# Attention and a LoRA mixture of experts: the products with V in three groups per head pair, of three, three and two key blocks, in place of four groups of two

## What is computed

```python
xq, xk, xv = x @ wq.T, x @ wk.T, x @ wv.T            # 16 heads of 32
scores = einsum("bqhd,bkhd->bhqk", xq, xk)
out = einsum("bhqk,bkhd->bqhd", softmax(scores), xv)
x = layernorm(x + out @ wo.T)
...
logits = x @ Wr.T + br
h = einsum("nd,erd->ner", x, A); y = einsum("ner,eor->neo", h, B) / 64
x = layernorm(x + y[argmax(logits)] * max(softmax(logits)))
```

## Time and profile before

| | us |
|---|---|
| median of 3 runs | 1507.79 |
| lowest and highest | 1507.14, 1510.0 |
| the profiled execution | 1506.31 |
| its span, from first to last instruction | 1504.5 |

### The profile page before, as it was taken

One profiled execution on the slowest core, in us unless ns is written; L12 is line 12 of the kernel. 1 busy time (PEld: TensorE's weight loads), 2 busy tenths in 40 slices (PEclk: granted clock), 3 DMA queues, 4 the chain that ended last, 5 costly groups with the idle time before them and its releaser, 6 DMA issues.

```text
span 1504.5 us, 21331 instructions
## 1 busy us (share of the span) xinstructions
PE 1444.2 (96%) x7176; PEld 909.3 (60%) x7176; DVE 976.8 (65%) x1850; ACT 784.7 (52%) x1430; POOL 1143.6 (76%) x651
## 2 busy tenths in 40 slices
PE   7999999999999999999999999999999999999997
PEld 5745556666645666666555666666664565565376
DVE  6747666666566677665556667666556777775564
ACT  3455556655455456455555546545554555555332
POOL 0376879888887779887779888879777899999311
PEclk9999999999999999999999999999999999999999
DMA  7345736574443434345353435234464112220001
GB/s 225 99 139 149 229 95 190 162 218 120 148 169 105 128 100 120 99 148 192 95 185 106 141 106 147 66 106 142 132 162 156 39 44 60 65 51 23 22 1 57
DMA packets 93661, 178.37 MB, mean 119 GB/s; under 512 B 19680, under 2 KB 35056, under 8 KB 92656
## 3 DMA queue, kind: packets, MB, share of 16 engines
q1 hardware_dynamic: 70240, 133.46, 31.2%
q10 hardware_dynamic: 22976, 42.47, 8.2%
q0 software_dynamic: 336, 1.07, 0.3%
HBM read 119.30 MB, written 56.88 MB: 117 GB/s over the span
## 4 chain that ended last, share of the span: by engine, by line
PE 82%; DVE 7%; issue 5%; POOL 3%; DMA 2%; ACT 1%; SPq 1%; ACTq 0%; POOLq 0%; DVEq 0%
PE w L697 24%; PE pv L856 15%; PE sc L844 14%; PE mx L834 13%; PE w L741 6%; DVE mxc L1156 3%; PE mx L808 3%; POOL Psum L596 2%; PE mx L697 1%; PE mx L768 1%; PE w L749 1%; DMA qk_parts<-split 1%; PE sc L697 1%; PE mx L757 1%; DVE stats L1245 1%
## 5 line engine op out<-in xcount | busy, mean ns | idle before, releaser
L1156 DVE TENSOR_REDUCE mxc<-mx 128x1 f32<-128x512 f32 x1024 | 682.7, 686 | 399.3 <-PE mx L834 396.6
L1001 ACT ACTIVATE P<-sc 128x512 f32<-128x512 f32 x1024 | 602.1, 597 | 483.9 <-PE sc L844 461.9
L596 POOL TENSOR_TENSOR Psum<-Psum,P 128x1024 f32<-128x1024 f32 x286 | 674.2, 2386 | 26.6 <-ACT P L1001 24.9
L844 PE MATMUL sc<-stack 98*128 98x512 f32 x1024 | 461.8, 453 | 5.8 <-ACT P L1001 4.9
L834 PE MATMUL mx<-stack 96*128 96x512 f32 x1024 | 406.9, 402 | 11.6 <-DVE eq L1295 4.9
L844 PEld LDWEIGHTS sc<-stack 98*128 98x128 f32 x1024 | 193.6, 189 | 97.0 <-issue 36.2
L834 PEld LDWEIGHTS mx<-stack 96*128 96x128 f32 x1024 | 195.1, 191 | 89.9 <-issue 27.6
L856 PE MATMUL pv<-P,V 128*32 128x512 f32 x2048 | 249.0, 604 | 0.0
L593 POOL TENSOR_TENSOR Psum<-P 128x1024 f32<-128x1024 f32 x50 | 118.8, 2392 | 114.4 <-ACT P L1001 88.8
L697 PE MATMUL w<-xT_s,wqk_s 128*128 128x512 f32 x504 | 161.5, 412 | 10.8 <-DVE xT_s L1172 10.8
L856 PEld LDWEIGHTS pv<-P,V 128*32 128x32 f32 x2048 | 56.6, 110 | 128.0 <-issue 102.4
(11 more groups left out here) (172 smaller groups left out, 1270.1 us busy)
## 6 DMA issues: line engine op xcount, KB each, us to landing
stack<-qk_parts SPq DMA_DIRECT2D x186, 256.0 KB, 4.4
qk_parts<-split SPq DMA_DIRECT2D x56, 512.0 KB, 3.5
wqk_s<-wqk_parts SPq DMA_DIRECT2D x40, 512.0 KB, 4.1
den_s<-den_parts SPq DMA_DIRECT2D x124, 64.0 KB, 2.0
r_f<-x ACTq DMA_DIRECT2D x3, 2048.0 KB, 12.6
wide<-a_parts ACTq DMA_DIRECT2D x3, 2048.0 KB, 8.0
out<-r_f SPq DMA_DIRECT2D x12, 512.0 KB, 3.4
xT_s_f<-xT ACTq DMA_DIRECT2D x5, 1024.0 KB, 8.3
```

What stands on the lines that cost most here:

```text
L596: pool.tensor_tensor(sums(s)[:, i, :], sums(s)[:, i, :], P[:, unit % NP, :], ALU.add).then_inc(add_done, 1)
L844: pe.matmul(sc[c][:, :], stack(s, i)[0:KS, 0, 128 * kb:128 * kb + 128], stack(s, i)[0:KS, 1, 512 * c:512 * c + 512], start=True, stop=True ...
L1001: act.activation(P[:, unit % NP, 512 * c:512 * c + 512], sc[c][:, :], ACT.Exp).then_inc(exp_done, 1)
L1156: dve.tensor_reduce(mxc[:, q % 2, at:at + 1], BANK["max", g][:, :], AX.X, ALU.max).then_inc(mx_done, 1)
```

## The change

The function that gives the blocks of a half is replaced by a table over the half in the slot: blocks 0, 1 and 2 at half 12, blocks 3, 4 and 5 at half 24, and, as before, blocks 6 and 7 at half 3 of the next slot (written as 35 of its own). The products, their operands and their semaphores stay. The groups of 12 and 24 stand in the first half of a unit, those of 11 and 19 stood in the second. Where `second` changes from one slot to the next, `den_at` goes from 11 to 12 (slots 25 to 28, 30 and 31); where it was 11 because of s % PAIRS == 2 alone (slots 10 and 18) it stays at 11. The steps at fixed distances from it follow.

```diff
--- before.py
+++ after.py
@@ -218,12 +218,14 @@
     def den_at(s):
 
 
-        return 6 if s <= PAIRS or s % PAIRS == 5 else 11 if second(s) != second(s - 1) or s % PAIRS == 2 else 3
-
-
-    def blocks(s, k):
-
-        return ((k - 5) // 2, (k - 3) // 2) if k % 4 == 1 and k >= 5 else ()
+        return 6 if s <= PAIRS or s % PAIRS == 5 else 12 if second(s) != second(s - 1) else 11 if s % PAIRS == 2 else 3
+
+
+    GROUPS = {12: (0, 1, 2), 24: (3, 4, 5), HALVES + 3: (6, 7)}
+
+    def blocks(h):
+
+        return GROUPS.get(h, ())
 
 
 
@@ -880,19 +882,17 @@
                     max_t(s + 1)
                 if s and half % HALVES == den_at(s):
                     den(s - 1, 0)
-                if c == 1 and s:
-                    for kb in blocks(s - 1, UNITS + k):
-                        if kb < KB:
-                            out_block(s - 1, kb)
-                if c == 1:
-                    for kb in blocks(s, k):
-                        out_block(s, kb)
+                if s:
+                    for kb in blocks(HALVES + half % HALVES):
+                        out_block(s - 1, kb)
+                for kb in blocks(half % HALVES):
+                    out_block(s, kb)
                 if half in X_PASS:
                     xi(*X_PASS[half])
                 for kind, n, chunk in AT.get(half, ()):
                     bank = begin((kind, n), False) if chunk == 0 else BANK[kind, n]
                     KIND[kind](n, chunk, bank)
-            for kb in blocks(LAST, UNITS + 1):
+            for kb in blocks(HALVES + 3):
                 out_block(LAST, kb)
             pe.wait_ge(exp_done, 2 * UNITS * SLOTS)
             pe.wait_ge(mx_done, max(FREES.values()))
```

## The result

The changed kernel takes 1521.71 us (median of 4 runs, 1519.79 to 1522.82), the kernel before on the same chip 1507.47 (4 runs, 1504.99 to 1510.0). The ratio is 1.0086, 95% interval 1.0066 to 1.0107: 13 us slower, where 6.7 us faster was forecast. The profiled execution of after is 1521.56, span 1519.8; before's was 1506.31, span 1504.5. The mean granted clock is 0.984 of full speed in after's trace and 0.993 in before's.

A forecast was written before the change was run, and what follows sets the result against it. The prediction took TensorE to set the pace. Its terms (-11.5 + 0.7 + 2.2 + 2.5 + 1.2 - 1.0 - 0.8) gave -6.7 us on 1506.31, 1499.6, or 1501.1 as median; range 1495 to 1506.5.

The forecast's parts named there:

- (a): TensorE: three groups a slot instead of four, each saving 0.36 us of entering and leaving narrow products, -11.5 us.
- rival F: TensorE's groups: the 0.36 us belongs to blocks, not groups, so that saving falls away; 1512.6 us, chance 0.02.
- (b): Dens of slots 10 and 18 stand alone at half 11, +0.7 us; in six other slots they stay joined.
- (c): New waits inside or behind the moved groups, on exponentials, buffers and V's tiles: cost nothing.
- (g): Group at 24 lets VectorE catch up before the maxima's transpose at half 26, -1.0 us.
- (h): Slots 15 and 23, halves from 24 on: longer group in front fills part of TensorE's waits, -0.8 us.
- (d): Chain over GpSimd gets shorter time, so dens of slots 9, 14 and 22 wait longer, +2.2 us.
- Rival D: GpSimd becomes the bound through the den in ten slots, 12.1 us instead of 2.2; 1511.0 us, chance 0.08.
- (e): Maximum banks: logit and transposed tiles lose the cover of groups at 19 and 27, net +2.5 us.
- (f): Slot 3, x passing through the maximum banks, loses the time the group at 19 gave VectorE, +1.2 us.
- Rival C: VectorE starves under groups of 2.91 us, holding at most three banks of work; 1505.4 us, chance 0.15.
- Rival E: Clock: waits of slots 9 and 14 grow and one more slow stretch costs 1.6 us; 1502.7, chance 0.03.

The follow-up runs named there:

- b2: Kernel before with reciprocals' store ahead of the stack load, maxima's transpose at half 24, and LEAD 5 for 4: 1506.29 us, ratio 0.998.
- best2: Changed kernel with reciprocals' store ahead of the stack load, maxima's transpose at half 24 before the group, and LEAD 5 for 4: 1496.94 us, ratio 0.9923.
- k24: Kernel before with only its third group moved, blocks 4 and 5 at half 24 instead of 27: 1523.51 us, ratio 1.0115.
- sp: Changed kernel with the reciprocals' store ahead of the stack load where both fall on half 14: 1517.83 us, ratio 1.0052.
- g27s: g27 with the reciprocals' store issued ahead of the stack load: 1506.49 us, ratio 0.998.
- g27: Changed kernel with its second group cut in two, block 3 at half 24, blocks 4 and 5 back at 27: 1518.06 us, ratio 1.0081.
- bsp: Kernel before with the reciprocals' store issued ahead of the stack load: 1504.35 us, ratio 0.9955.
- b24: Kernel before with the maxima's transpose at half 24 instead of 26, from slot 2 on: 1520.05 us, ratio 1.0102.
- best: Changed kernel with the maxima's transpose inside the group at half 24, behind block 3, and reciprocals' store ahead of the stack load: 1501.31 us, ratio 0.9936.

## Why the prediction was wrong, step by step

**Price of a group, (a): right, a little too large.** TensorE of after in slot 17, a half with three blocks:

```profile
801.06 0.80 PE L846 MATMUL sc<-stack 98*128 98x512 f32 x1
...
802.02 2.78 PE L858 MATMUL pv<-P,V 128*32 128x512 f32 x24
...
805.30 0.80 PE L846 MATMUL sc<-stack 98*128 98x512 f32 x1
```

4.24 us, 2.91 above the 1.33 of a plain half beside it, as forecast. By whole slots the saving is a little smaller. Slots 17 and 25, where neither chain shows, went from 44.84 to 44.55 and from 44.83 to 44.51 us: 0.3 each, and b2 against best2 gives 0.29. So (a) is about -9.6 in place of -11.5, and rival F, that the price belongs to blocks, falls.

**(b): right.** The lone dens of slots 10 and 18 make halves of 2.36 and 2.37 us, as the earlier trace rows.

**(c): this is the step that failed.** It asked what each group waits for and who waits for its blocks, and never what other work had run under the group at its old place. It is true that no product with V waits. But a group is also 2 us in which TensorE has work and waits for none of the others, and every chain that leaves TensorE before it and comes back behind it is shorter of time by that when the group goes. Two chains crossed the old places: maxima from half 26 to 32 over the group at 27 (13.1 us of wait, k24), and store, load, store, split from 13 to 23 over the group at 19 (ScalarE's wait +13.0, TensorE's wait for exponentials +2.1; 3.5 us in slot 5 by sp, more in g27s). The two don't add up: 17 us (k24) and 12 (g27) less the 9.6 saved would be 20 and not 13. That a wait in one chain gives time to the other would explain it, but is not shown. The first was one step away: (g) priced the transpose at half 26 as one that receives from VectorE, and did not follow what it starts. The trace before even showed it, with 0.31 us of wait in slot 16 and so no spare; the prediction has no term for it. (h) has the wrong sign for the same reason: the ends of slots 15 and 23 were called halves short of work on ScalarE's account, but just because they hold so little work, they are where the maxima's way is least covered: slot 15 +2.67, slot 23 +3.78.

**(d): too large where it was named, and of the wrong sign in total.** The den of slot 9 waits 2.31 us where 3.2 was forecast, that of slot 14 0.16 for 0.8. TensorE of after at these dens, and GpSimd in slot 8:

```profile
417.44 1.06 PE L810 MATMUL mx<-Psum,ones 128*32 128x512 f32 x8 [2.31 <-POOL Psum L598]
...
652.12 1.07 PE L810 MATMUL mx<-Psum,ones 128*32 128x512 f32 x8 [0.16 <-POOL Psum L598]
```

```profile
398.15 2.64 POOL L632 TENSOR_TENSOR attT_f<-pv_s,den_s 64x512 f32<-64x512 f32 x2 [2.17 <-issue]
```

GpSimd stands 2.17 us ahead of the normalise and not 3.00: the backlog did not start the whole 0.85 later. In total the waits for GpSimd fell from 5.2 to 3.7, -1.5 for the +2.2 forecast: the ones of slots 11 and 19, 1.05 and 2.23 us before, are 0 and 0.63 now, a new one of 0.60 stands in slot 23, and (d) had taken all slots but 9, 14 and 22 for unchanged. Rival D falls with it. That a chain through these reciprocals matters was right, and bsp shows it from the other side: two steps of SyncE reordered took 4 of the 5.2 us away.

**(e): right in kind, too large.** The waits of `max_item` for `eq` and `turned` (L1188) grew from 4.9 and 3.7 to 6.1 and 4.8, new ones at slot 26 half 21, slot 27 half 29 and slot 29 half 21; others, 0.9 us ahead of the den in slot 28 and 0.4 in slot 26, are gone. Net +1.0 for the 2.5; no new one stands in slots 18 and 19. **(f)**: x passed through in slot 3 with 1.3 us of waits, 1.2 before, so nothing in place of 1.2. **(g)**: the transpose at half 26 waits 5.5 us in all for 6.8, -1.3 in place of -1.0. **Rival C**, that VectorE starves, is not seen: its busy time went from 976.8 to 978.7 us, and its idle time before L1156 from 399 to 409, less than the span grew. **Rival E**, the clock: given 0.03 and one stretch of 1.6 us. It was about half of the result. The stand that it feared, slot 14, measured 0.16 us; slot 9's 2.31 us was followed by full clock this time (1.00 from 417.4 to 421.0), and five of after's eight falls in the loop came at stands that no step had. The upper ends in the sum come to 1508.9, or 1511.1 with the six dens of (b), and not to 1510.3, which changes nothing above.

The account, in waits of the two traces: -9.6 (a) + 0.6 (b) - 1.5 (d) + 1.0 (e) - 1.3 (g) + 13.1 maxima + 2.1 exponentials + 0.7 for a product that waits for x - 0.4 for the smaller rest (all of TensorE's waits went from 52.7 to 66.4, +13.7) = 4.7. For the clock: over 27 runs of before on one chip, the time rises by 10.6 us for each 0.01 that the mean granted clock falls (0.996 at 1503.5, 0.985 at 1513.6; 0.990 on the mean, 0.992 on the mean of 13 runs on another chip); after's four runs have 0.984 on the mean, 0.006 to 0.008 less, some 6 to 9 us by this estimate, which is taken across chips. Together 11 to 14, where 13 to 14 was measured. The two traces alone give 4.7 + 11.9 for the clock = 16.6 against 15.3.

## What to carry to other kernels

Before a long block of one engine is moved, list every chain that leaves that engine before the block's old place and comes back after it, through every other engine and DMA queue, and read how much of it is hidden under the block; a wait of 0.3 us there says that no cover is spare. Where a chain has lost its cover, start it earlier, ahead of the block, rather than put the block back: best2 kept the cheaper groups and moved the starts. First see that what the chain starts from is ready by then (b24: 15 us lost). And try a small store that someone waits for ahead of a large load on the same queue: it helped in three kernels here (before, after and g27).

## What the runs showed of the hardware that was not expected

**The clock differs from one execution to the next of the same kernel.** Before's runs lie between 0.985 and 0.996, and 10 us apart with them, with the same program on the same chip; the profiled one (0.993) was a favourable one. Which stand is followed by a fall isn't settled. In after, the ones of 3.85, 3.10 and 2.62 us were, and so were a stretch of slot 29 behind waits of no more than 0.86 and one of slot 18 behind 0.73; before's three falls in the loop stand behind 1.58, 0.53 and 1.97. The den of slot 9 waits longer in after (2.31) and is followed by full clock. But the idle of 2.1 us in slot 26 half 1, behind which after falls, stands in before too and is followed by full clock. The Trainium skill ("TensorE: Matmul & The Clock Gate", section "Why this matters for your kernels") wants idle gaps between bursts of matmuls kept short; the trace agrees for the two longest, 3.85 and 3.10. The gaps that it warns of are longer than all the others here, so the rule doesn't tell the short ones apart, nor those of the earlier trace rows.

**Entering narrow products costs, and only once.** A group costs about 0.3 us, be it of two blocks or three, and a den of the same shape joins it for no more than its products (the earlier trace rows and the 2.91 above). A transpose set inside a group adds little: slot 17 took 44.55 us in after and 44.69 in best, 0.14 more. That this is the group entered a second time is not shown, because in b24, with no group at half 24, the earlier transpose adds 0.16 to the same slot.

**A small store behind loads on one queue.** The store of the reciprocals (8 KB) held up the next issue for 4.42 us when 768 KB of loads stood before it, and for 1.80 us, with those loads issued in between, when it went first (after and sp, slot 5).
